# Layers 2 and 3 of a fused transformer kernel: the mix of probabilities and values with high and low halves side by side, and the score block moved behind the step's projections

## What is computed

```
x = x + _L2_xattn_ref(_layernorm(x, axis=-1), ctx_768, ...)     # layer 3 likewise

q = (x @ Wq).reshape(B, N, HEADS, DIM_HEAD).transpose(0, 2, 1, 3)
k = (context @ Wk).reshape(B, M, HEADS, DIM_HEAD).transpose(0, 2, 1, 3)
v = (context @ Wv).reshape(B, M, HEADS, DIM_HEAD).transpose(0, 2, 1, 3)
dots = jnp.einsum('bhnd,bhmd->bhnm', q, k) * SCALE
attn = jax.nn.softmax(dots, axis=-1)
out = jnp.einsum('bhnm,bhmd->bhnd', attn, v)
return out @ Wo + bo
```

## Time and profile before

| | before |
|---|---|
| median of 3 runs | 1894.32 us (1894.15 to 1895.41) |
| the profiled execution | 1890.68 us, of which its span 1888.9 us |
| PE busy | 1775.6 us (94%) |
| DVE busy | 1382.2 us (73%) |
| ACT busy | 1017.8 us (54%) |
| POOL busy | 496.5 us (26%) |
| granted TensorE clock, mean | 0.982 of full |

### The profile page before, as it was taken

One profiled execution on the slowest core, in us unless ns is written; L12 is line 12 of the kernel. 1 busy time (PEld: TensorE's weight loads), 2 busy tenths in 40 slices (PEclk: granted clock), 3 DMA queues, 4 the chain that ended last, 5 costly groups with the idle time before them and its releaser, 6 DMA issues. The chain is left out here.

```text
span 1888.9 us, 31069 instructions
## 1 busy us (share of the span) xinstructions
PE 1775.6 (94%) x11692; PEld 1574.6 (83%) x11695; DVE 1382.2 (73%) x3118; ACT 1017.8 (54%) x2239; POOL 496.5 (26%) x522
## 2 busy tenths in 40 slices
PE   6869999999999999999977999999979999999698
PEld 6658898999999898999856888888867888888587
DVE  6478787878777787878685575757777777777786
ACT  4455555565555565555554464646623666666421
POOL 0613030302112030303001333333521433334242
PEclk9988999999999999999999999999989999999899
DMA  5100000000000000000021212020000000000111
GB/s 172 67 17 26 1 12 1 6 7 1 12 1 12 1 12 1 15 1 1 1 89 51 69 45 83 30 70 10 9 1 18 21 12 15 9 10 4 35 52 36
DMA packets 17749, 49.05 MB, mean 26 GB/s; under 512 B 2617, under 2 KB 7362, under 8 KB 15938
## 3 DMA queue, kind: packets, MB, share of 16 engines
q1 hardware_dynamic: 16738, 46.25, 7.4%
q10 hardware_dynamic: 864, 0.83, 0.1%
HBM read 46.15 MB, written 0.92 MB: 25 GB/s over the span
## 5 line engine op out<-in xcount | busy, mean ns | idle before, releaser
L1381 ACT ACTIVATE a_pH<-banks 125x512 fp32r<-125x512 f32 (+1 forms) x384 | 203.5, 544 | 268.0 <-PE banks L195 191.4
L1452 DVE TENSOR_TENSOR a_pL<-banks,a_pH 125x512 fp32r<-125x512 f32 (+1 forms) x384 | 235.4, 623 | 116.7 <-ACT a_pH L1381 114.8
L2000 POOL TENSOR_TENSOR a_prob<-a_prob,a_rinv 112x750 f32<-112x750 f32 x128 | 184.0, 1437 | 394.4 <-DVE a_rinv L2311 394.4
L1433 DVE TENSOR_SCALAR_CACHE_REDUCE a_prob<-banks 128x500 f32<-128x500 f32 x336 | 221.8, 676 | 5.0 <-PE banks L195 4.1
L1271 PE MATMUL banks<-ident,a_prob 128*125 128x128 f32 x1344 | 201.2, 274 | 6.6 <-ACT a_prob L1366 4.4
L1366 ACT ACTIVATE a_prob<-a_prob,a_nmax 128x1000 f32<-128x1000 f32 x168 | 187.9, 1121 | 32.8 <-DVE a_nmax L1436 32.8
L195 PE MATMUL banks<-a_pH,a_head_vH 125*128 125x256 f32 (+1 forms) x576 | 200.1, 347 | 5.2 <-DVE a_pL L1452 4.3
L1271 PEld LDWEIGHTS banks<-ident,a_prob 128*125 128x125 f32 x1344 | 186.4, 188 | 9.8 <-ACT a_prob L1366 4.9
L1225 POOL TENSOR_TENSOR a_head_oH<-a_o,ones 128x256 fp32r<-128x256 f32 (+1 forms) x24 | 16.4, 684 | 605.8 <-DVE a_o L1460 605.8
L195 PE MATMUL banks<-a_pH,a_head_vL 125*128 125x256 f32 (+1 forms) x576 | 173.1, 300 | 0.0
L195 PE MATMUL banks<-a_pL,a_head_vH 125*128 125x256 f32 (+1 forms) x576 | 172.5, 300 | 0.0
(11 more groups left out here) (414 smaller groups left out, 5065.8 us busy)
## 6 DMA issues: line engine op xcount, KB each, us to landing
a_w_out<-in_f_out SPq DMA_DIRECT2D x6, 1024.0 KB, 5.0
a_w_in<-in_f_in SPq DMA_DIRECT2D x12, 512.0 KB, 4.8
f_raw<-in_f_w SPq DMA_DIRECT2D x9, 513.0 KB, 3.6
pair_raw<-in_a_qk SPq DMA_DIRECT2D x16, 256.0 KB, 2.8
pair_raw<-in_a_w SPq DMA_DIRECT2D x8, 384.0 KB, 3.1
a_v<-in_ctx_rows SPq DMA_DIRECT2D x4, 576.0 KB, 7.7
a_kT<-in_f_w SPq DMA_DIRECT2D x2, 1024.0 KB, 5.8
pair_raw<-in_a_wv SPq DMA_DIRECT2D x8, 256.0 KB, 3.0
```

What stands on the lines that cost most here:

```text
L1381: act.activation(pH[:, c % RING, 0:wide], TB[c % 4][0:KB, 0:wide], ACT.Copy).then_inc(t_high, 1)
L1433: dve.tensor_scalar(prob[:, at, c * CHUNK:(c + 1) * CHUNK], SB[c % 3][:, 0:CHUNK], SCALE, None, ALU.mult, ALU.max, accum_out=chunk_max[:, ...
L1452: dve.tensor_tensor(pL[:, c % RING, 0:wide], TB[c % 4][0:KB, 0:wide], pH[:, c % RING, 0:wide].bitcast(F32), ALU.subtract).then_inc(t_done, 1)
L2000: pool.tensor_tensor(both, both, rinv[:, n % RING, :].unsqueeze(2).to_broadcast([SEQ, 2, KEYS]), ALU.mult).then_inc(p_normed, 1)
```

## The change

Three things, all inside `attention_heads64`, so in layers 2 and 3.

1. **The mix.** The values are laid out so that 128 neighbouring columns hold the high and the low part of one head, and the probabilities so that the high and low part of one head are 224 neighbouring columns of the moving operand. Per head and key tile one matmul gives vH\*pH, vH\*pL, vL\*pH and vL\*pL: six matmuls of 224 columns for nine. Their results lie in different quarters of OB, so putting them together changes: ACT copies vL\*pH (two of 64x112) to `o_small`, crossing from one half of the partitions to the other; DVE adds vH\*pH and vH\*pL with a reduce over pairs (two, reading 64x224) into `o_main`; and POOL, in a new `cut_mixed`, adds both, makes oH and then oL (three operations of 128x112 in a row).
2. **The score block.** PE no longer begins step n with scores(n+3), but has scores(n+4) behind the items of step n and ahead of mix(n). The start of the layer gets one more block. The lists of ACT and DVE keep their order.
3. **The second half of the queries** moves from step 8 (step 0 of the next pair) to step 7.

```diff
-    QUERIES_AT = (3, 8)
+    QUERIES_AT = (3, 7)
...
-        vH = sb("vH", [KB, KTILES, 2 * P], F32R)
-        vL = sb("vL", [KB, KTILES, 2 * P], F32R)
+        v = sb("v", [KB, KTILES, 4 * P], F32R)
...
-        pH = sb("pH", [KB, 2, BKT * PAIR], F32R)
-        pL = sb("pL", [KB, 2, BKT * PAIR], F32R)
-        bias = sb("bias", [P, D])
+        p = sb("p", [KB, 2, 2, BKT * PAIR], F32R)
+        o_parts = sb("o_parts", [P, 2, 2, SEQ])
+        o_main, o_small = o_parts[:, 0], o_parts[:, 1]
...
+        def mixed(i):
+            return OB[:, i * 2 * SEQ:(i + 1) * 2 * SEQ].rearrange("p (s c) -> p c s", s=2)
...
+            def cut_mixed(n):
+                tok = slice((n % BATCH) * SEQ, (n % BATCH + 1) * SEQ)
+                whole = o_main[:, n % 2, :]
+                pool.wait_ge(main_out, n + 1)
+                pool.tensor_tensor(whole, whole, o_small[:, n % 2, :], ALU.add).then_inc(o_summed, 1)
+                pool.wait_ge(o_summed, n + 1)
+                pool.tensor_copy(oH[:, tok], whole).then_inc(o_high, 1)
+                pool.wait_ge(o_high, n + 1)
+                pool.tensor_tensor(oL[:, tok], whole, oH[:, tok].bitcast(F32), ALU.subtract).then_inc(o_done, 1)
...
                     if n + 2 < STEPS:
                         norm(n + 2)
+                    if n >= 1:
+                        cut_mixed(n - 1)
...
-                need(pe, o_done, n)
-                terms = []
-                for k in range(BKT):
-                    t, p_high, p_low = BKT * b + k, pH[:, n % 2, k * PAIR:(k + 1) * PAIR], pL[:, n % 2, k * PAIR:(k + 1) * PAIR]
-                    terms += [(vH[:, t, mine], p_high), (vL[:, t, mine], p_high), (vH[:, t, mine], p_low)]
-                split_products(pe, OB[:, 0:PAIR], terms).then_inc(pv_done, 1)
+                need(pe, main_out, n)
+                for i in range(2):
+                    mine = slice((2 * (h % 2) + i) * P, (2 * (h % 2) + i + 1) * P)
+                    last = split_products(pe, OB[:, i * 2 * SEQ:(i + 1) * 2 * SEQ], [
+                        (v[:, BKT * b + k, mine], p[:, n % 2, :, k * PAIR + i * SEQ:k * PAIR + (i + 1) * SEQ])
+                        for k in range(BKT)])
+                last.then_inc(pv_done, 1)
 
             def step(h, b):
                 n = BATCH * h + b
-                if n + AHEAD < STEPS:
-                    scores(*divmod(n + AHEAD, BATCH))
                 if n + 1 < STEPS:
                     turn(n + 1)
...
+                if n + AHEAD + 1 < STEPS:
+                    scores(*divmod(n + AHEAD + 1, BATCH))
                 mix(h, b)
...
             def outputs(n):
-                tok = slice((n % BATCH) * SEQ, (n % BATCH + 1) * SEQ)
                 act.wait_ge(pv_done, n + 1)
+                need(act, o_summed, n - 1)
                 for i in range(2):
-                    rows = slice(i * HD, (i + 1) * HD)
-                    last = act.activation(oH[rows, tok], OB[rows, i * SEQ:(i + 1) * SEQ], ACT.Copy)
-                last.then_inc(o_high, 1)
+                    rows, others = slice(i * HD, (i + 1) * HD), slice((1 - i) * HD, (2 - i) * HD)
+                    last = act.activation(o_small[rows, n % 2, :], mixed(i)[others, :, 0], ACT.Copy)
+                last.then_inc(small_out, 1)
...
             def outputs(n):
-                tok = slice((n % BATCH) * SEQ, (n % BATCH + 1) * SEQ)
-                dve.wait_ge(o_high, n + 1)
+                dve.wait_ge(small_out, n + 1)
+                need(dve, o_done, n - 1)
                 for i in range(2):
                     rows = slice(i * HD, (i + 1) * HD)
-                    last = dve.tensor_tensor(oL[rows, tok], OB[rows, i * SEQ:(i + 1) * SEQ],
-                                             oH[rows, tok].bitcast(F32), ALU.subtract)
-                last.then_inc(o_done, 1)
+                    last = dve.tensor_reduce(o_main[rows, n % 2, :], mixed(i)[rows], AX.X, ALU.add)
+                last.then_inc(main_out, 1)
```

More of the change, by code:

```diff
@@ L1828, in queries_at @@
     def queries_at(h, b):
-        return [(h, n) for n, at in enumerate(QUERIES_AT) if at == b + BATCH] \
-            + [(h + 1, n) for n, at in enumerate(QUERIES_AT) if at == b and h + 1 < HEADS]
+        return [(0, 1)] * (h == 0 and b == 0) + [(h + 1, n) for n, at in enumerate(QUERIES_AT) if at == b and h + 1 < HEADS]
     def outs_at(h, b):
@@ L1949, in chunk, with value_parts, projected @@
             return slice(c * CHUNK, (c + 1) * CHUNK)
+        def value_parts(u):
+            parts = v[:, UNIT * u:UNIT * u + UNIT, :].rearrange("p t (j s d) -> p (t j) s d", s=4, d=HD)
+            return parts[:, :, 0:4:3, :], parts[:, :, 1:3, :]
+        def projected(m):
+            return bank(m)[0:KB, :].rearrange("p (j i d) -> p j i d", i=2, d=HD)
+        def mixed(i):
+            return OB[:, i * 2 * SEQ:(i + 1) * 2 * SEQ].rearrange("p (s c) -> p c s", s=2)
         block = ctx.enter_context(nc.Block())
@@ L1973, in expert @@
                 sp.dma_start(w_in[:], dram["f2_in"][e, j]).then_inc(in_loaded, 16)
-            sp.dma_start(bias[:], dram[f"a{layer}_bias"]).then_inc(bias_loaded, 16)
+            sp.dma_start(bias, dram[f"a{layer}_bias"]).then_inc(bias_loaded, 16)
             outs(0)
@@ L2050, in _ @@
                         cut_values(h // 2 + 1)
+            cut_mixed(STEPS - 1)
         @block.tensor
@@ L2183, in _ @@
                 values(0, u)
+            scores(0, 3)
             for h in range(HEADS):
@@ L2202, in values @@
             def values(j, u):
-                item("v", j, u, vH[:, UNIT * u:UNIT * u + UNIT, :],
-                     bank(number["v", j, u])[0:KB, :].rearrange("p (t c) -> p t c", t=UNIT))
+                item("v", j, u, value_parts(u)[0], projected(number["v", j, u]))
             def exps(n):
@@ L2284, in values @@
             def values(j, u):
-                m = number["v", j, u]
-                tiles = slice(UNIT * u, UNIT * u + UNIT)
+                v_high, v_low = value_parts(u)
                 dve.wait_ge(high, highs["v", j, u] + 1)
-                dve.tensor_tensor(vL[:, tiles, :], bank(m)[0:KB, :].rearrange("p (t c) -> p t c", t=UNIT),
-                                  vH[:, tiles, :].bitcast(F32), ALU.subtract).then_inc(done, 1)
+                dve.tensor_tensor(v_low, projected(number["v", j, u]), v_high.bitcast(F32), ALU.subtract).then_inc(done, 1)
             def outs(h, g):
```

15 lines of the change are left out of this document (9 added, 6 removed).

## The result

| | before | changed |
|---|---|---|
| median of 13 runs each | 1892.65 us (1890.35 to 1895.41) | 1897.27 us (1896.20 to 1902.69) |
| ratio | | 1.0028, 95% interval 1.0020 to 1.0037 |
| the profiled execution | 1890.68 us, span 1888.9 | 1898.94 us, span 1897.1 |
| PE, DVE, ACT, POOL busy | 94, 73, 54, 26% | 92, 74, 54, 34% |
| granted clock, mean | 0.982 | 0.975 |

The account below looks back on a forecast made before the run. PE's own instruction list was taken to bound the kernel (busy 265.64 of 266 us). Frames +1.9 and layer ends +3.0 sum to +4.9 us, which on the median of 1894.3 gives 1899.2 us; range 1888 to 1909.

Parts of the forecast that it names:

- The floor moves: Shortest time from one step's last pair of scores to the next: from 3.60 to 4.35 us.
- A frame that PE fills: Time between successive last pairs of scores, where PE's work sets it: 0.29 us shorter, 0.333 saved less 0.04.
- Frames in sum: 126 intervals between last pairs of scores, each the longer of PE time and 4.35: +1.9 us, 53 at 4.35.
- The queries: Second half's projection moves 1.20 us from step 0 to step 7; step 0 also loses its wait, 0.13 a pair.
- The layer ends: From last scores to DVE's last work in each layer: 13.1 us becomes 14.6, +1.5 a layer, +3.0.
- The clock costs nothing: PE's granted clock stays at 1.00 though a step 0 idles 1.35 of 4.35 us: no cost.
- my third rival: Clock falls to 1.2 GHz in step 0's holes, about 1.6 us longer on 13 frames: +21, 1920 us; chance 0.03.
- Costed at nothing: DVE's longer outputs (+0.23 us) and POOL's three operations (1.4 us) in mid-layer: covered, no cost; DVE's cover 0.3 us.

Follow-up runs that it names:

- The mix alone: The kernel before with only the new six-matmul mix, PE's order and the queries as before: 1870.54 us, ratio 0.9881.
- the block alone: The kernel before with scores at each step's end, four batches ahead, and queries at step 7, still nine matmuls: 1936.94 us, ratio 1.0232.
- the two statements turned about: The changed kernel with PE doing the mix first and then the scores four batches ahead: 1869.50 us, ratio 0.9875.
- the two traces where the holes are filled: The changed kernel plus useless matmuls where PE idles: in steps 2 and 3 of each layer's last pair, 1895.99 us; at four places of each layer, 1894.84 us.
- the two doublings: The changed kernel with POOL's subtraction for oL done twice, 1899.20 us; with each of DVE's two reduces done twice, 1908.73 us.
- the queries at step 8: The changed kernel with the second half of the queries back at step 8: 1901.75 us, ratio 1.0047.
- ACT's order turned about: The changed kernel with ACT doing the exponentials before the copy of the transposed probabilities to pH: 1910.88 us, ratio 1.0092.

## Why the prediction was right, point by point

The forecast was 1899.2 us, +4.9 on the kernel before, and the measurement is 1897.27, +4.6. The mechanism is the one named: the order on PE raises the floor. That the total came within 0.3 us is luck, since terms were off and offset each other: the frames came out some 5 us lower than summed, the layer ends and the clock some 6 us higher.

- *The floor moves.* Forecast 4.35; it is 4.26 to 4.30. The copy to pH starts 1.90 behind the last pair, not 1.95, and the last pair of scores starts 0.41 behind the first as given. On 52 frames (forecast 53) this 0.05 to 0.09 is about -4 us. The mix alone (3.60), the block alone (4.60, three matmuls more) and the two statements turned about (3.60) show that the move of the floor comes from the order.
- *A frame that PE fills.* Forecast -0.29; it is -0.30 to -0.33.
- *Frames in sum.* Forecast +1.9; they gave -1.8, and -3.6 without the 1.8 us that the clock cost in the last frame. The floor accounts for 4 us of the difference, and the rest is in the filled frames.
- *The queries.* Step 7 got 0.92 longer, as forecast (1.20 less 0.29), and step 0 came to the floor. Their wait did not go, and I had misread its size: of the 17 times and 8.1 us 13 times and 5.4 us are weight loads, and PE itself waited 2.7 us in 4 times. With the change PE's own are these:

```profile
PE banks L2139 <- DVE a_qL L2306: 4.5, 3, 2.1
```

They stand at the starts of the two layers, where the second half is projected right ahead of the scores that need it. The frames that hold the two long ones are 4.99 and 5.00 us, as before, so this wait cost nothing by itself. Without the move the kernel would be some 4 us slower.
- *The layer ends.* Forecast +1.5 each. In the two traces where the holes are filled they are 15.5 for 13.1, so +2.4. The convention of my sum counts a mix as over when its sixth matmul starts; by it the four turnarounds of OB take 10.0 us (forecast 9.6, so the turnaround was mis-sized by 0.1 each), ACT and DVE behind the last mix 1.65 (1.66), POOL 1.34 (1.4), and the output projection with its addition 1.54 (1.1). This last term is the clock's too. The projection before, and with the holes filled:

```profile
1378.20 0.36 PE L195 MATMUL banks<-a_woH,a_oH 128*128 128x256 f32 x1 [0.54 <-issue]
1376.27 0.56 PE L195 MATMUL banks<-a_woH,a_oH 128*128 128x256 f32 x1 [1.48 <-issue]
```

From the end of the cut of the outputs to DVE's last work it is 1.15 before and with the block alone, and 1.54 in every trace with the new mix, where PE has stood idle for 1.5 us and more at a time behind the last mixes and runs it at a granted clock of 0.50. So 0.4 of each end is the lower clock even where the holes are filled, and without it the ends grew by 2.0. The two parts of the change don't add up at the ends: +1.8 with the mix alone and +2.4 with the block alone, but +2.4 with both, since most of the block's 2.4 was the clock.
- *The clock costs nothing.* **This step failed.** I took its level from a stretch in which PE was busy 6.31 of 8 us and applied it to frames that idle 2.0 of 4.3. It fell at both layers' ends and cost about 5 us in the profiled execution: 1.8 in the last frame, 1.0 and 1.5 at the ends, and twice 0.4 in the last projection. Filling the holes at the ends took the first three away in the trace, 4.2 us, and lowered the median by 2.7 us, and by 4.4 in the session where the holes at the starts were filled too. But it did not fall in the holes of step 0 (idle 1.3 of 4.3), as my third rival had it: the 1470 to 1736 us window shows 1.00. The Trainium skill ("TensorE: Matmul & The Clock Gate", Part 4) says that transposes do not count as PE busy in the same way as other matmuls. The runs here don't tell that apart from idle time, since each frame where the clock fell has both; but six transposes in every frame of the middle of a layer went with 1.00.
- *Costed at nothing.* DVE and POOL in the middle of a layer: right, by the two doublings. The reduce is 0.386 us (forecast 0.39 to 0.40), and POOL's three operations 0.42, 0.28 and 0.42.

That the kernel ends up near where it was is a sum of large terms of both signs: 31 us less of PE work, and 38 us more of waiting at the scores.

## What to carry to other kernels

When an engine's list is rearranged, write down for the shortest loop what stands between a result and its return (here: scores, ACT's outputs, copy, exponentials, scores), and see which producers the move has put inside it. The saved matmuls were worth 22 us with the old order and were lost in the new one, and the exchange of two statements in one engine's list shows it. And a shorter engine doesn't stop at the wait that was planned for: each version here ran into the next one, so list the waits by how far behind the bound they are.

## What was not expected of the hardware

At the ends of the layers the granted clock fell from 1.00 to 0.50 behind one or two frames of 4.3 us in which PE had idled 2.0 us each, and it stayed at 1.00 through hundreds of us of frames with 1.3 us of idle time in some. In between, the length of a hole alone does not say what happens. Behind a single hole of 2.1 us at the start of layer 3 it fell in three traces (the kernel with the end filled and the two with a doubled operation) and not in four others (the changed kernel twice, the block alone and the queries at step 8). Behind the same hole at the start of layer 2 it fell in none of the seven. Behind holes of 1.7 us it fell four times of five (ACT's order turned about), behind one of 1.5 us once (scores behind the mix) and with the mix alone at the same place not at all. What else decides stays open. A fall cost 0.7 to 2.1 us in the frames it hit, through matmuls at half speed (the mix 1.62 for 0.93, the transposes 1.46 for 0.81), and where useless matmuls filled the holes it did not fall.
